# Late expert groups of the first batch flipped into two bank sets in turn in an AdaLN and mixture-of-experts FFN kernel

## What is computed

```
c      = (x @ cond_B[itok].T) @ cond_A[itok].T                 # rank 16
base   = c @ base_w.T + base_b
res    = c @ ffn_A.T                                           # rank 64
probs  = softmax(c @ router_w.T)                               # 16 experts
topw, topi = top_k(probs, 2);  topw = topw / (sum(topw) + 1e-6)
combine    = sum_k one_hot(topi_k) * topw_k
delta  = einsum('bse,bsr,eor->bso', combine, res, ffn_B)
out    = x + base + 0.5 * delta
```

## Time and profile before

| | us |
|---|---|
| median of 3 runs | 446.51 |
| lowest and highest of them | 444.71, 446.59 |
| the profiled execution, own time | 445.62 |
| its span in the profile | 443.8 |
| TensorE busy in the span | 409.7 (92%) |
| VectorE busy | 319.4 (72%) |
| ScalarE busy | 108.1 (24%) |

### The profile page before, as it was taken

One profiled execution on the slowest core, in us unless ns is written; L12 is line 12 of the kernel. 1 busy time (PEld: TensorE's weight loads), 2 busy tenths in 40 slices (PEclk: granted clock), 3 DMA queues, 4 the chain that ended last, 5 costly groups with the idle time before them and its releaser, 6 DMA issues.

```text
span 443.8 us, 6785 instructions
## 1 busy us (share of the span) xinstructions
PE 409.7 (92%) x2496; PEld 279.9 (63%) x2496; DVE 319.4 (72%) x830; ACT 108.1 (24%) x163; POOL 40.5 (9%) x53
## 2 busy tenths in 40 slices
PE   0597997999788999999999999999999999999996
PEld 0475985656556766666667666666666676666665
DVE  2699996999468496668677875966686778756453
ACT  0003114435473231123113112311231131123110
POOL 4020000002100120012001201200120012012000
PEclk9999998999999999999999999999999999999999
DMA  8999999999999999899999999998999898556935
GB/s 223 357 330 331 334 357 366 345 269 336 289 295 239 352 362 323 279 349 342 310 287 378 306 315 302 366 312 295 348 335 325 285 366 303 207 201 217 343 128 189
DMA packets 75027, 135.35 MB, mean 305 GB/s; under 512 B 5506, under 2 KB 14770, under 8 KB 74994
## 3 DMA queue, kind: packets, MB, share of 16 engines
q1 hardware_dynamic: 56000, 102.08, 69.7%
q10 hardware_dynamic: 18994, 32.84, 23.5%
HBM read 99.23 MB, written 35.65 MB: 304 GB/s over the span
## 4 chain that ended last, share of the span: by engine, by line
PE 63%; DVE 10%; DMA 9%; SPq 6%; POOL 3%; ACT 3%; issue 3%; ACTq 2%; POOLq 0%; DVEq 0%
PE ps L927 13%; PE ps L928 11%; PE ps L929 11%; PE ps L901 11%; PE ps L941 6%; DMA bexpT<-in_x 6%; PE ps L930 5%; POOL u_r L480 3%; DMA gm_r<-xT 3%; DVE xT L728 3%; DVE early L659 3%; SPq L296 3%; ACT bexpT L495 2%; PE ps L856 2%; PE ps L949 2%
## 5 line engine op out<-in xcount | busy, mean ns | idle before, releaser
L840 DVE TENSOR_TENSOR xbuf<-ps,xbuf 128x512 f32<-128x512 f32 x128 | 86.7, 677 | 96.0 <-PE ps L930 96.0
L927 PE MATMUL ps<-h_r,u_r 128*128 128x512 f32 x256 | 108.8, 425 | 0.7
L928 PE MATMUL ps<-h_r,u_r 128*128 128x512 f32 x256 | 100.3, 392 | 0.0
L929 PE MATMUL ps<-h_r,u_r 128*128 128x512 f32 x256 | 100.1, 391 | 0.0
L866 PE MATMUL ps<-early 128*128 128x256 f32 x256 | 66.5, 408 | 22.6 <-DVE early L659 22.6
L728 DVE STREAM_TRANSPOSE xT<-xbuf 128x256 f32<-128x256 f32 x224 | 80.6, 410 | 0.0
L866 PEld LDWEIGHTS ps<-early 128*128 128x128 f32 x256 | 48.1, 201 | 36.8 <-issue 16.5
L927 PEld LDWEIGHTS ps<-h_r,u_r 128*128 128x128 f32 x256 | 48.1, 188 | 35.9 <-issue 16.7
L659 DVE STREAM_TRANSPOSE early<-xbuf 128x256 f32<-128x256 f32 x128 | 65.9, 577 | 5.3 <-issue 3.8
L901 PE MATMUL ps<-bexpT,cur 128*32 128x512 f32 x512 | 61.6, 598 | 2.2 <-DVE h_r L707 1.5
L495 ACT ACTIVATE h_r<-ps 128x512 fp32r<-128x512 f32 x64 | 36.2, 595 | 78.8 <-PE ps L901 78.4
(11 more groups left out here) (67 smaller groups left out, 205.3 us busy)
## 6 DMA issues: line engine op xcount, KB each, us to landing
out<-xbuf SPq DMA_DIRECT2D x31, 1024.0 KB, 7.3
xbuf<-in_x SPq DMA_DIRECT2D x28, 1024.0 KB, 7.4
xbuf<-in_x ACTq DMA_DIRECT2D x32, 512.0 KB, 10.9
xbuf<-in_x SPq DMA_DIRECT2D x32, 512.0 KB, 8.6
xbuf<-in_L_ffn_base_w SPq DMA_DIRECT2D x16, 512.0 KB, 19.3
xbuf<-in_L_ffn_base_w ACTq DMA_DIRECT2D x16, 512.0 KB, 20.1
gm_r<-g_hilo SPq DMA_DIRECT2D x128, 32.0 KB, 6.8
early_u<-in_L_ffn_B SPq DMA_DIRECT2D x10, 256.0 KB, 18.5
```

The lines of the kernel that those rows point to most:

```text
L840: dve.tensor_tensor(xs, ps[:, tile_bank(b.n, m), :], xs, ALU.add).then_inc(s_out, 1)
L927: pe.matmul(acc, u_r[:, b.q, 0, h, tok_t], hi, start=(h == 0), stop=False)
L928: pe.matmul(acc, u_r[:, b.q, 0, h, tok_t], lo, start=False, stop=False)
L929: pe.matmul(acc, u_r[:, b.q, 1, h, tok_t], hi, start=False, stop=False)
```

## The change

Among the late groups, 11 and 13 are flipped into banks 6 and 7 (`MISC` and the bank behind it), the others stay in banks 0 and 1. Each flip waits only for the copy of the group that used its banks last (`E_BEFORE`): group 11 waits for none, 12 for group 10, 13 for group 11, 14 for groups up to 12, 15 for groups up to 14. Group 14 is flipped after tile 4 and not after tile 5, and its copy moves with it in ScalarE's order. The first `bx_products` of batch 1, which write bank 7, get a wait until group 13 is copied.

```diff
@@ -214,7 +214,8 @@
-        E_LATE = {0: 10, 1: 11, 2: 12, 3: 13, 5: 14, 6: 15}
+        E_LATE = {0: 10, 1: 11, 2: 12, 3: 13, 4: 14, 6: 15}
+        E_BEFORE = {10: 10, 11: 0, 12: 11, 13: 12, 14: 13, 15: 15}
@@ -225,7 +226,9 @@
         def e_bank(g):
 
-            return EB if g >= len(E_AT) or g % 2 else HB
+            if g >= len(E_AT):
+                return MISC if g in (11, 13) else EB
+            return EB if g % 2 else HB
@@ -869,7 +872,7 @@
             def expert_flips(g):
 
                 pe.wait_ge(s_ein[E_SLOT[g]], 32 * (len(e_users(g)) + 1))
-                need(pe, s_ec, g - 1 if g < len(E_AT) else g)
+                need(pe, s_ec, E_BEFORE[g] if g >= len(E_AT) else g - 1)
@@ -935,6 +938,8 @@
                     if k == 0:
                         need(pe, s_up, f.n * 2)
+                        if f.n == 1:
+                            pe.wait_ge(s_ec, 14)
                         pe.wait_ge(s_bsel, NB)
```

## The result

| | before | changed |
|---|---|---|
| median of the six executions beside each other | 446.55 us | 460.31 us |
| lowest and highest | 444.71, 458.64 | 458.04, 464.88 |
| profiled execution, own time | 445.62 | 458.62 |
| its span | 443.8 | 456.8 |

The ratio is 1.0337, 95% interval 1.0256 to 1.0418: slower by 3.4%, where 0.6% faster was forecast. One thing has to be known to read the numbers: executions of one and the same kernel come out near 445 us or some 5 to 25 us later (the kernel before was at 452 us or more in 38 of the 115 that ran beside the experiments), so every kernel is given with its median, its lowest and highest and how many executions were at 452 or more, and the ratio leaves out the two of the kernel before that were.

What follows compares the result with a forecast made beforehand. TensorE, 92% busy, was taken as the bound, with the lap flip, copy, flip bounding 121 to 129 us. A gain of 2.5 from 445.62 gave 443.1, from the median 444.0; forecast 443.6 us, range 441.6 to 445.6.

Steps and rivals of the forecast that it cites:

- Parts 1 to 4: Batch 0: flips 13 end 2.71 us earlier; bx_products wait 0.66; flips 15 end 2.67 earlier; tile 7 waits 0.72.
- the sum of 2.5 us: Net gain forecast from batch 0's late flips, taken off the profiled 445.62 us.
- the lap of the flips: TensorE's lap over flips of groups 11 to 13 without waits: 0.89 + 1.62 = 2.51 us.
- The cover of tile 3: Tile 1's add ends at 123.83, tile 3 starts at 124.12: 0.3 us to spare.
- Rival 1: All waits at the late flips go: the whole 3.7 us return, 441.9 or 442.8 us; chance 1 in 10.
- part 5: Batch 0's products for block 3 start at 140.49, 2.44 us earlier, and later batches keep the shift.
- Rival 3: Moved 1 MB x reload delays other DMAs; 4.4 us of cover, slower over 9.1, perhaps 450 us; chance 0.05.

Runs made afterwards that it cites:

- e15: The changed kernel with SP's residual reload of block 3 issued behind its half of the next x, not ahead of it; median 444.51 us.
- e17: The kernel of e15 once more, with twelve executions; median 444.0 us.
- e18: The kernel before, without the flips' change, with SP's reload of block 3 issued behind x; median 445.39 us.
- e5: The changed kernel with 1.75 MB of SP's half of batch 2's transposed x left out; median 443.55 us.
- e2: The changed kernel with eleven extra matmuls, about 2.5 us, ahead of batch 0's products for block 3; median 446.24 us.
- e13: The changed kernel with ScalarE's half of the next x issued at tiles 6 and 10, not 4 and 8; median 444.82 us.
- e3: The kernel before without the second matmul of each half in tiles 8 to 13 of batch 0; median 452.92 us.

## Why the prediction was wrong

**Parts 1 to 4 held, and the sum of 2.5 us nearly.** Put on the changed kernel's clock (0.52 us earlier): the lap of the flips was given as 2.51 us and was 2.48; bx_products were to start at 128.62 and did at 128.78; tile 7 at 138.15, it was 138.23; the products for block 3 at 139.97, they came at 140.12. Their start moved by 2.29 us from flips 10 on, where 2.44 was worked out. By batch 1's first tile 2.03 are left (2.55 less 0.52): the bx_products of tile 8 took 2.01 us (141.97 to 143.99 in the chain) and not 1.73 as before. The cover of tile 3, called 0.3 us thin, may have cost 0.1 us: its first matmul has 0.36 us in the chain and not 0.23, with no wait listed. The copies took 6.75 us for three; the sum had 6.58. Rival 1, that all waits go, fell for the reason given there: ScalarE's order.

**The step that failed is in part 5**: "Behind that I see nothing that eats it", and "everything in them hangs on what went before, so a shift there is kept". TensorE's share of a later batch was read as proof that it is the bound. The same rows have a DMA share of 0.96, and the loop store, reload, add, which sets its own pace, was not priced. Its parts stood in the trace of the kernel before: stores that landed after 4.1 to 13.7 us, reloads after 5.1 to 13.9. With a store of 21.65, a reload of 11.63, 7.8 until the fourth add is done and 2.3 of SP's it needs 43.35 us, 2.65 more than TensorE's batch. A shift to earlier is kept only if what shares the path can follow. 2.5 us of TensorE's lead is, as an estimate, about 0.8 MB at 322 GB/s that the DMA engines had to move earlier; in the changed kernel block 3's store was not down in time, SP was held, and the halves of x parted. In e15 and e17, where SP isn't held ahead of x, the same lead is kept to the end of the profile.

**Rival 3 named the queue and missed the mechanism.** It priced one late reload: 4.4 us of cover for batch 1's first add, slower only from 9.1 us. That cover held; no add of batches 1 or 2 waits for a DMA. What it left out is that a late transfer delays the issue of the next ones, and that the transfers then run in another mixture, in which they move fewer bytes: 286 to 306 GB/s and not 322 to 324, as the windows have it. Because of that the loss did not stop at what was moved (3.5 us) but went on at 2 to 6 us a batch. Its chance, 0.05, was worked out as if cover were all that counted. The rule cited with it, from the Trainium skill's page DMA: Bandwidth & Descriptors, section Issuing engines are not separate DMA queues, agrees with the trace as far as it goes. The same page of the Trainium skill, section Queues, rings and completion order, says that on each DMA engine the descriptors of one queue are taken up in order, and that the engine goes round between queues; the store at 173.43 has up to 2 MB of reloads and 1 MB of x ahead of it on SP's queue and 1 MB on ScalarE's, and lands after 21.6 us, at most 243 GB/s for the five MB with its own. That agrees with the order; the low rate is not in these rules but in the windows.

**The range was too narrow for a second reason.** The three runs of the kernel before lay within 1.9 us, and I took that for its spread. Executions of it 5 to 25 us later were not in the three. The profile could have warned, with a DMA share of 0.94 to 0.98 from 160 to 360 us, but the share alone would not have told: e18 has 0.99 there and no late execution.

**What stays open** is why x of one queue alone moves at 215 GB/s, and what decides, in one execution and not in the next, whether block 3's store is down in time. That less owed work (e5), a later TensorE (e2) or another order (e13, e15) keeps the halves of x together in the profiles is shown; the property of the DMA engines behind the rates is not.

## What to carry to other kernels

Before a gain on one engine is called kept, price the loop of transfers that the stage feeds, store, landing, reload, landing, next use, against the new pace, and look at what is in flight together: here a lead of 2.5 us cost 13 in one profile. A wait for a landing belongs behind the transfers that are ready, not ahead of them, where one engine issues both in order. Time a kernel that runs its DMA engines full more often than three times before a change of half a per cent is judged.

## What the runs showed of the hardware that was not expected

The DMA engines moved less while they were busy all the time: 286 to 314 GB/s at a share of 1.04 to 1.06 in the changed kernel's windows of 40 us from 160 to 360, 321 to 327 at 0.94 to 0.98 in those of the kernel before, for the same bytes and packets. But the share doesn't tell the rate. e13 moves 324 to 336 GB/s at 1.04 to 1.05 in the same windows, the first of them:

```profile
160.00:200.00 40.00, 39.88 (x255) 25.94 (x254) 29.17 (x84) 8.61 (x16) 4.03 (x4) 1.00 1.05 329
```

What differs is which transfers run side by side: 215 GB/s for x of one queue, 302 for x of both. In e3 the median of four executions was 7 us above that of the kernel before (452.92 against 445.58) with 2.7 us of matmuls left out. And an issue can hold the engine that makes it: SP's four issues of g rows, 1.9 us at 176 in the kernel before, took 8.06 us at 174 in the changed one, with up to 5 MB issued ahead of them and not landed.
